# Flamingo gated block on one core: the heads' sums leave through DRAM untransposed, and their division is done for eight heads at a time

## The chip, the cores and the metric

The kernel runs on one core of one Trainium2 chip. The metric is the device time of one execution in microseconds (us). A core has a matrix engine (TensorE, "PE"; its weight loads, "PEld", overlap its matmuls), three engines for elementwise work (VectorE "DVE", ScalarE "ACT", GpSimd "POOL"), and a queue that issues transfers (SyncE, "SP"); they run at the same time and wait for each other by semaphores. The matmuls read SBUF and write PSUM, of which there are eight banks of 128 x 512 float32.

## The reference

Four sequences of 512 tokens with 256 channels go through gated attention and a gated mixture of experts. Cut to what matters here:

```python
xn = layernorm(x)
for each of 4 sequences and 16 heads (D = 16 channels each):      # 64 heads
    y  = softmax(q  k^T  * scale + causal) @ v                      # 512 keys
    y += softmax(qc kc^T * scale) @ vc                              # 1601 keys of the context
x  = x + tanh(g_xattn) * (concat(y) @ Wp + bp)
xn = layernorm(x)
out = x + tanh(g_ffn) * (shared_expert(xn) + sum of the top 2 of 7 routed experts, weighted)
expert(h) = (silu(h @ g.T) * (h @ u.T)) @ d.T                       # inner width 704
```

Each softmax has its own denominator, so a head ends with two numerators and two denominators for each of its 512 queries.

## The kernel before

**Stages.** The preparation (0 to 138 us) makes the queries and keys of all heads as stacks of three bfloat16 pieces and stores them to DRAM (`q_parts`, `k_parts`). The head loop (138 to 923) does the 64 heads one after the other. Then come the turning of y, the projection, the residual, the second layernorm, the shared expert and the routing, and the routed experts.

**A head step.** Scores are computed with keys on partitions and queries along the free axis, in eight groups (L651, L654). ACT exponentiates each group (L993). The values phases (L669) multiply the exponentials by a stack of values with a column of ones, in four groups of 32 PSUM partitions: three groups sum parts of the cross attention, the fourth the self attention. So after a head, PSUM bank 6 holds on partitions 32q to 32q+15 the numerators of part q (a channel each), and on partition 32q+16 its denominator, along 512 queries. `sums_out` (ACT, L974) copies that bank to `osb` in SBUF.

**The division, per head.** `norm` (PE, four transposes, L718) turns `osb` so that queries lie on partitions; `norm_out` (ACT, L982) copies it out; `cross_sums` (POOL, L1133 and L1135) adds the three cross parts; `reciprocals` (DVE, L1326) inverts the 128 x 8 denominators; `head_output` (POOL, L1125 and L1128) multiplies and writes the head's 16 columns of y into `shared`. After the last head, 32 transposes (L540) and eight ACT copies (L1015) bring y into the layout that the projection (L760) wants, channels on partitions: `xnT`.

**Maxima of the next heads.** A softmax needs a maximum ahead of its exponentials. PE computes bounding score pieces of the two following heads, 16 "max pieces" a head (L551 to L566), and DVE reduces each (L1242). From the first half of a head's pieces and the second, `max_parts` (DVE, L1254 to L1260) makes the row of maxima; it is transposed by PE (`rows`, L592), copied by ACT into `rowst` (L953), and put by an SP transfer (`rows_load`, L471) into the stack from which the scores of the next head are made. The pieces, `norm` and `rows` take turns in a ring of three PSUM banks (`ENTRIES`, `RING`); each waits until what used its bank three entries ago is evacuated (`bank_free`).

**Order.** Every engine has its program written out by hand. `PE_ORDER` sets PE's order in a step: with group 3 of the scores come values phase 0 and `norm`, with group 5 come `rows` and values phase 1. `run_steps` writes steps 0 and 1, a loop of 15 turns of four heads, and two more steps. SP issues, once the scores of a head are done, six transfers for the stack of the head four further on (L461), then `rows_load`.

## Time and profile before

| | us |
|---|---|
| median of 3 runs | 1413.0 (1412.93 to 1413.5) |
| the profiled execution | 1413.27 |
| its span in the trace | 1411.5 |
| PE busy in the span | 1368.6 |
| DVE, ACT, POOL busy | 880.9, 727.3, 365.4 |

The span is that of the trace from the first to the last instruction; the time that is reported contains 1.8 us more. Busy times of different engines overlap. An engine that is busy the whole span has to lose work, or to lose waits, for the time to fall; for the others it only matters when they finish what is waited for.

### The profile page before, as it was taken

The numbers are of one execution on the slowest core, as the hardware profiler recorded it, in microseconds if no ns is written. First come the engines' busy times: TensorE is split into PE (matmuls) and PEld (weight loads), VectorE is DVE, ScalarE is ACT, GpSimd is POOL, SyncE is SP. The second block draws the span as 40 slices with busy tenths as digits, with TensorE's granted clock in tenths as the row PEclk, the third lists the DMA queues.
The fourth block names the chain that finished last, engine by engine and source line by source line (L and its number), as shares of the span: only waits on it lengthen the run. The fifth ranks groups of instructions, "written<-read, shape, count | busy, mean of one in ns | idle before, by whom it ended". The sixth has DMA issues, their size and how long they took to land.

```text
span 1411.5 us, 27301 instructions
## 1 busy us (share of the span) xinstructions
PE 1368.6 (97%) x7688; PEld 694.0 (49%) x7689; DVE 880.9 (62%) x1804; ACT 727.3 (52%) x1107; POOL 365.4 (26%) x743
## 2 busy tenths in 40 slices
PE   7988999999999999999999999989999999999997
PEld 4544333333333333333333333364556777777775
DVE  6776888888888888888888888653532222222221
ACT  4644667677777676767676767732210222222221
POOL 5655222222222222222222222200001232233232
PEclk9999999999999999999999999999999999999999
DMA  8754111111111111111111111057004122112111
GB/s 246 237 186 154 43 53 51 48 50 48 47 49 50 51 50 50 49 48 48 48 51 51 50 49 50 7 218 297 0 1 134 26 33 34 30 30 37 30 30 23
DMA packets 57711, 98.43 MB, mean 70 GB/s; under 512 B 7441, under 2 KB 42001, under 8 KB 56657
## 3 DMA queue, kind: packets, MB, share of 16 engines
q1 hardware_dynamic: 50384, 88.10, 18.8%
q0 software_dynamic: 7296, 9.97, 4.5%
q8 instruction: 15, 0.25, 0.1%
q14 instruction: 16, 0.12, 0.0%
HBM read 69.20 MB, written 28.58 MB: 69 GB/s over the span
## 4 chain that ended last, share of the span: by engine, by line
PE 88%; DMA 2%; DVE 2%; ACT 1%; issue 1%; POOL 1%; SPq 0%; POOLq 0%; ACTq 0%; DVEq 0%
PE ps L669 19%; PE ps L834 13%; PE ps L651 13%; PE ps L551 13%; PE ps L847 7%; PE ps L786 5%; PE ps L797 3%; PE ps L718 3%; PE ps L654 2%; PE ps L565 2%; PE ps L858 2%; DMA k_parts<-work 2%; PE ps L555 1%; PE ps L592 1%; PE ps L625 1%
## 5 line engine op out<-in xcount | busy, mean ns | idle before, releaser
L1242 DVE TENSOR_REDUCE mx<-ps 128x1 f32<-128x512 f32 (+1 forms) x832 | 515.1, 662 | 99.6 <-PE ps L551 69.3
L993 ACT ACTIVATE arena<-ps 128x1024 f32<-128x1024 f32 (+1 forms) x512 | 484.3, 995 | 138.7 <-PE ps L651 135.2
L669 PE MATMUL ps<-arena 128*32 128x512 f32 (+5 forms) x2432 | 290.9, 525 | 0.6 <-ACT arena L993 0.4
L551 PE MATMUL ps<-arena 96*128 96x512 bf16 x768 | 263.0, 382 | 7.3 <-DMA arena<-k_parts 2.9
L651 PE MATMUL ps<-arena 98*128 98x512 bf16 x832 | 264.4, 381 | 5.0 <-DMA arena<-rowst 4.9
L1144 POOL TENSOR_SCALAR_AFFINE_SELECT arena<-arena 128x128 f32<-128x128 f32 x256 | 74.8, 292 | 439.2 <-ACT arena L993 429.3
L834 PE MATMUL ps<-arena,work 128*128 x608 | 186.4, 460 | 0.6 <-issue 0.6
L551 PEld LDWEIGHTS ps<-arena 96*128 96x128 bf16 x768 | 74.1, 96 | 178.0 <-DVE mx L1242 103.2
L1520 DVE TENSOR_TENSOR work<-work,ps 128x352 f32<-128x352 f32 x76 | 39.6, 521 | 179.1 <-ACT work L1061 179.1
L834 PEld LDWEIGHTS ps<-arena,work 128*128 128x128 f32 x608 | 112.5, 190 | 57.4 <-issue 1.1
L1242 DVE TENSOR_REDUCE mneg<-ps 128x2 f32<-128x512 f32 (+2 forms) x192 | 112.4, 640 | 23.9 <-PE ps L561 23.4
L1061 ACT ACTIVATE work<-ps 128x352 f32<-128x352 f32 x76 | 35.2, 463 | 164.6 <-PE ps L834 164.6
L1186 POOL DMA_INDIRECT out<-bv,slot_table x38 | 59.9, 1575 | 207.3 <-DVE bv L1526 197.5
L669 PEld LDWEIGHTS ps<-arena 128*32 128x32 f32 (+1 forms) x2432 | 56.6, 108 | 113.1 <-issue 110.5
L651 PEld LDWEIGHTS ps<-arena 98*128 98x128 bf16 x832 | 76.5, 98 | 66.2 <-DMA arena<-rowst 6.1
L847 PE MATMUL ps<-arena,work 128*128 (+1 forms) x456 | 105.0, 379 | 0.8 <-ACT work L1067 0.8
L847 PEld LDWEIGHTS ps<-arena,work 128*128 128x128 f32 (+1 forms) x456 | 83.6, 190 | 11.4 <-issue 1.1
L1176 POOL DMA_INDIRECT wp<-xn_rows,slot_table x38 | 37.7, 993 | 173.5 <-DVE slot_table L1509 137.7
L1066 ACT ACTIVATE work<-ps 128x256 f32<-128x256 f32 x76 | 29.0, 382 | 99.7 <-PE ps L858 99.6
L786 PE MATMUL ps<-xnT,arena 128*128 128x512 f32 x176 | 77.1, 595 | 0.4 <-DVE work L1352 0.4
L654 PE MATMUL ps<-arena 98*128 98x512 bf16 (+3 forms) x256 | 66.1, 299 | 0.0
L1526 DVE TENSOR_SCALAR bv<-ps,router 128x256 f32<-128x256 f32 x38 | 18.4, 484 | 64.1 <-PE ps L847 64.1
(161 smaller groups left out, 1406.8 us busy)
## 6 DMA issues: line engine op xcount, KB each, us to landing
arena<-in_experts SPq DMA_DIRECT2D x8, 2176.0 KB, 12.2
arena<-k_parts SPq DMA_DIRECT2D x64, 198.1 KB
arena<-k_parts SPq DMA_DIRECT2D x64, 132.1 KB
arena<-q_parts SPq DMA_DIRECT2D x64, 96.0 KB
k_parts<-work SPq DMA_DIRECT2D x16, 300.0 KB, 5.2
q_parts<-work SPq DMA_DIRECT2D x12, 384.0 KB, 5.4
arena<-k_parts SPq DMA_DIRECT2D x64, 66.0 KB
arena<-q_parts SPq DMA_DIRECT2D x64, 64.0 KB
```

Of the source, the lines that this page charges most:

```text
L551: mm = pe.matmul(out, qx[:, qt * P:(qt + 1) * P], ks[0:KROWS, T + j * CHUNK:T + (j + 1) * CHUNK], start=True, stop=True)
L651: mm = pe.matmul(bk[:, 0:w], kst[r][0:KROWS + MROWS, T + kt * P:T + (kt + 1) * P], qst[r][0:KROWS + MROWS, 1, :], start=True, stop=True)
L654: mm = pe.matmul(bk[:, o0:o0 + w], kst[r][0:KROWS + MROWS, kt * P:(kt + 1) * P], qst[r][0:KROWS + MROWS, 0, kt * P:T], start=True, stop=True)
L669: mm = pe.matmul(ps[32 * q:32 * q + VW, 6, b0:b1], vst[0:kn, r % VR, TT + kt if cross else kt, :], pr[0:kn, c0:c0 + b1 - b0], start=(phase ...
L718: mm = pe.transpose(out[:, t * P:(t + 1) * P], osb[:, t * P:(t + 1) * P], ident[:, :])
L786: mm = pe.matmul(ps[:, 2 * (k0 % 2) + j, :], wgus[:, k, w0:w0 + P], xnT[:, k, tb * T:(tb + 1) * T], start=(k == 0), stop=(k == 1))
L834: mm = pe.matmul(ps[:, 2 * c + j, 0:CH], xgT[:, b, k, :], weights[:, bass.ds(e, 1), o:o + CH], start=(k == 0), stop=(k == 1))
L847: mm = pe.matmul(ps[:, 4, 0:C], hidT[0:m, it, :], weights[0:m, bass.ds(e, 1), o:o + C], start=(it == 0), stop=(it == IT - 1))
L993: act.activation(pr[:, c0:c0 + n], ps[:, 2 * (g % 2):2 * (g % 2) + 2, :].rearrange("p b n -> p (b n)")[:, 0:n], ACT.Exp, scale=SCALE).then ...
L1144: pool.affine_select(out=exps, in_=exps, pattern=[[1, P]], compare_op=ALU.is_ge, fill=0.0, base=0, channel_multiplier=-1).then_inc(S["mask ...
L1186: pool.indirect_dma_start(out=a["out"], out_offset=bass.IndirectOffsetOnAxis(slot_table[:, i, 1:2], 0), in_=yt[:, i % 2, :], in_offset=Non ...
L1242: return dve.tensor_reduce(m, out, AX_X, ALU.max)
```

## The change

1. `norm`, `norm_out` and the per-head `cross_sums`, `reciprocals` and `head_output` are gone. The entry of `norm` in the ring of banks stays as `spare`, so that no other piece changes its bank.
2. After each head, SP stores `osb` (256 KB) to a DRAM buffer `o_parts`; the next `sums_out` waits for that store (`o_written`).
3. Once for eight heads (which are 128 channels of one sequence, thus half of the projection's input), SP loads from `o_parts`: `parts_load`, eight transfers, four for the denominators as 128 x 32 tiles ("compactly": 8 heads x 512 queries on 128 partitions) and four for the numerators, 128 channels x 512 queries, one of them straight to the place of y in `xnT`. POOL adds the cross parts (`den_sums`, `num_sums`), DVE inverts the 128 x 64 denominators (`reciprocals`), SP stores them to DRAM (`recip_store`) and loads them again repeated over the 16 channels of each head (`recip_load`), and POOL makes y with three 128 x 512 operations (`outputs`). These steps lie in different heads of the next group: the load after the group's last head's `rows_load`, then `SUMS_IN` = 5, `RECIP_IN` = 6 and `OUT_IN` = 7.
4. Steps 0 to 3 are written out, then a loop of 7 turns of eight heads, then four steps more.
5. y is made in the projection's layout, so the 32 transposes and eight copies after the last head are gone, and the projection of sequences 0 to 2 stands right behind the last values phase; its sequence 3 waits for the last group's division. The order of PE there becomes: `project(0..2)`, `turn_xn(0)`, `shared_up(0)` pieces 0 to 3, `project(3)`, pieces 4 and 5, `turn_xn(1..3)`. ACT now issues the load of the shared expert and one store of normalised rows; SP issues the last group's transfers ahead of those of the routed experts.
6. The first `rows_load` is issued within the last stores of the preparation and no longer behind them.

```diff
 def schedule():
...
         if g == 3:
-            out += [("values", 0), ("norm",)]
+            out += [("values", 0), ("spare",)]
...
+GH = P // D
+NGRP = NU // GH
+BEGUN = GH // 2
+TURNS = NGRP - 1
+SUMS_IN, RECIP_IN, OUT_IN, RECIP_AT = 5, 6, 7, 3
...
 def run_steps(eng, step):
-    step(0, 0, False, True, True)
-    step(1, 1, True, True, True)
-    heads = NR
-    turns = (NU - 2 - 2) // heads
-    with eng.Fori(0, turns) as i:
-        for h in range(heads):
-            step(i * heads + (h + 2), (h + 2) % NR, True, True, True)
+    for u in range(BEGUN):
+        step(u, u % NR, u > 0, True, True)
+    with eng.Fori(0, TURNS) as i:
+        for h in range(GH):
+            step(i * GH + (BEGUN + h), h % NR, True, True, True, i, h)
...
@@ block.sync
+                if s == ROWS_LOAD_AT:
+                    rows_load(0, 0)
...
-            rows_load(0, 0)
...
+            def sums_store(v):
+                sp.wait_ge(S["o_evac"], v + 1)
+                sp.dma_start(o_parts[bass.ds(v, 1)].rearrange("a p t -> (a p) t"), osb).then_inc(S["o_written"], 16)
+            def parts_load(j):
+                sp.wait_ge(S["parts_free"], j + 1)
+                sp.wait_ge(S["o_written"], j * (16 * GH) + 16 * GH)
+                heads = o_parts[bass.ds(j * GH, GH)]
+                for q in range(4):
+                    src = heads[:, VW * q + D:VW * q + D + 1, :].rearrange("u a (d t) -> (u a) d t", t=DW)
+                    sp.dma_start(den[:, q, :], src).then_inc(S["parts_in"], 16)
+                for q, dst in enumerate([yT[:, bass.ds(j, 1), :].rearrange("p a t -> p (a t)"), *cross_num, self_num]):
+                    sp.dma_start(dst, heads[:, VW * q:VW * q + D, :]).then_inc(S["parts_in"], 16)
...
+                    stack_loads(i * GH + (BEGUN + NR + h), h % NR)
+                    sums_store(i * GH + (BEGUN + h))
+                    if h + 1 == OUT_IN:
+                        recip_load(i)
+                    rows_load(i * GH + (BEGUN + h + 2), (h + 2) % NR)
+                    if BEGUN + h == GH - 1:
+                        parts_load(i)
+                    if h + 1 == RECIP_IN:
+                        recip_store(i)
...
@@ block.tensor
-            def norm(u):
-                pe.wait_ge(S["o_evac"], u)
-                for t in range(TT):
-                    mm = pe.transpose(out[:, t * P:(t + 1) * P], osb[:, t * P:(t + 1) * P], ident[:, :])
...
-            pe.wait_ge(S["y_done"], NU)
-            for n in range(8):
-                layer_turn(ps[:, n % 4, :], b, k).then_inc(S["y_turned"], 1)
...
@@ block.scalar
             def sums_out(u):
                 act.wait_ge(S["pv_done"], u * NPH)
+                if not (isinstance(u, int) and u == 1):
+                    act.wait_ge(S["o_written"], u * 16 - 16)
...
@@ block.gpsimd
+            def outputs(j):
+                y = group_out(j)
+                pool.wait_ge(S["recip_in"], j * 32 + 32)
+                pool.tensor_tensor(y, y, cross_recip, ALU.mult).then_inc(S["y_cross"], 1)
+                pool.tensor_tensor(self_num, self_num, self_recip, ALU.mult).then_inc(S["y_self"], 1)
+                pool.tensor_tensor(y, y, self_num, ALU.add).then_inc(S["y_done"], 1)
```

On PE, in a step of the head loop, between values phase 0 and the max piece behind it, there stands before (L669 values, L718 `norm`, L551 a max piece, L651 scores):

```order
L669 MATMUL ps<-arena 32x512 x4
L577 REGISTER_ALU
L718 MATMUL ps<-ident,work 128x128 x4
L577 REGISTER_ALU
L551 MATMUL ps<-arena 128x512
L682 REGISTER_ALU
L651 MATMUL ps<-arena 128x512 x2
```

and now (L731 values, L614 a max piece, L713 scores):

```order
L731 MATMUL ps<-arena 32x512 x4
L641 REGISTER_ALU
L614 MATMUL ps<-arena 128x512
L744 REGISTER_ALU
L713 MATMUL ps<-arena 128x512 x2
```

Only the four transposes and one register operation are gone; the order of the rest of the step is the same, down to `rows` (now L654) and beyond.

On SP, at the step of the loop in which a group of eight is complete, there stood before, behind the six stack loads (the last one is shown), the `rows_load` and then the next stack loads:

```order
L461 DMA arena<-k_parts 16x2113
L470 REGISTER_ALU
L471 DMA arena<-rowst 2x8x128
L507 REGISTER_ALU
L461 ISA
L461 DMA arena<-q_parts 48x1x1024
```

and now the beginning of what stands there (L524 the store of the sums, L487 `rows_load`, L533 the loads of the denominators in `parts_load`, of which there are four):

```order
L524 DMA o_parts<-work 128x512
L487 DMA arena<-rowst 2x8x128
L528 REGISTER_ALU
L529 ISA
L533 ISA
L533 DMA work<-o_parts 128x1x32
L533 ISA
L533 DMA work<-o_parts 128x1x32
```

The rows above are the first two of the eight loads. The end of the same place, with the last two of the four numerator loads (L535) and the first load of the next stack (L477):

```order
L535 DMA shared<-o_parts 128x1x512
L535 ISA
L535 DMA work<-o_parts 128x1x512
L559 REGISTER_ALU
L477 ISA
L477 DMA arena<-q_parts 48x1x1024
```

The eight loads of a group come between the `rows_load` of one head and the stack loads of the next, where nothing stood before.

On PE behind the last values phase there stood before (L718 the last `norm`, L540 the transposes of y and of the normalised rows, L760 the projection, L786 the shared expert):

```order
L718 MATMUL ps<-ident,work 128x128 x4
L540 MATMUL ps<-ident,shared 128x128 x32
L760 MATMUL ps<-wp,xnT 128x256 x24
L540 MATMUL ps<-ident,shared 128x128 x8
L760 MATMUL ps<-wp,xnT 128x256 x8
L786 MATMUL ps<-xnT,arena 128x512 x22
L540 MATMUL ps<-ident,shared 128x128 x24
L786 MATMUL ps<-xnT,arena 128x512 x4
```

and now (L806 the projection, L603 the transposes of the normalised rows, L830 the shared expert):

```order
L806 MATMUL ps<-wp,xnT 128x256 x24
L603 MATMUL ps<-ident,shared 128x128 x8
L830 MATMUL ps<-xnT,arena 128x512 x16
L806 MATMUL ps<-wp,xnT 128x256 x8
L830 MATMUL ps<-xnT,arena 128x512 x6
L603 MATMUL ps<-ident,shared 128x128 x24
L830 MATMUL ps<-xnT,arena 128x512 x4
```

The last `norm` and the 32 transposes of y are gone, and the last eight matmuls of the projection moved behind 16 matmuls of the shared expert.

## Rows read from the trace of the kernel before

**Rows 1.** The page: busy us by engine (share of the span) x instructions.

```profile
PE 1368.6 (97%) x7688; PEld 694.0 (49%) x7689; DVE 880.9 (62%) x1804; ACT 727.3 (52%) x1107; POOL 365.4 (26%) x743
```

**Rows 2.** Windows: stretch, length, busy (x) by engine, PEclk, DMA share, GB/s.

```profile
150.00:900.00 750.00, 748.01 (x5129) 287.39 (x5127) 630.34 (x1222) 530.99 (x672) 178.90 (x548) 1.00 0.15 49
502.27:514.58 12.31, 12.27 (x87) 4.71 (x84) 10.26 (x20) 8.69 (x11) 2.94 (x9) 1.00 0.16 50
```

**Rows 3.** All instructions of L718, duration in ns min/median/max.

```profile
L718 PE MATMUL ps<-ident,work x256: 272/273/329, 157.9 to 924.0; 128*128 128x128 f32 x128
```

**Rows 4.** Timeline of two heads: start, length, engine, line, [idle before <-releaser].

```profile
502.69 2.54 DVE L1242 TENSOR_REDUCE mx<-ps 128x1 f32<-128x512 f32 x4 [0.32 <-PE ps L551]
...
512.41 1.75 DVE L1242 TENSOR_REDUCE mneg<-ps 128x2 f32<-128x512 f32 x3 [0.43 <-PE ps L561]
514.19 0.17 DVE L1254 TENSOR_REDUCE mneg<-mx 128x4 f32<-128x16 f32 x1
...
514.09 0.66 PE L718 MATMUL ps<-ident,work 128*128 128x128 f32 x4
...
514.58 0.38 PE L551 MATMUL ps<-arena 96*128 96x512 bf16 x1
...
515.00 2.54 DVE L1242 TENSOR_REDUCE mx<-ps 128x1 f32<-128x512 f32 x4 [0.23 <-PE ps L551]
...
516.39 0.09 PEld L592 LDWEIGHTS ps<-identb,mparts 128*16 128x16 bf16 x1 [0.30 <-DVE mx L1242]
```

**Rows 5.** Timeline of SP and PE in one head, and of the 61st.

```profile
505.11 0.68 SPq L471 DMA_DIRECT2D arena<-rowst  x1
507.15 0.77 SPq L461 DMA_DIRECT2D arena<-q_parts  x1
...
508.32 0.60 PE L651 MATMUL ps<-arena 98*128 98x512 bf16 x2
...
910.26 0.62 SPq L471 DMA_DIRECT2D arena<-rowst  x1
...
912.05 0.82 PE L651 MATMUL ps<-arena 98*128 98x512 bf16 x3 [0.30 <-DMA arena<-rowst]
```

**Rows 6.** POOL: all operations of L1111, duration in ns min/median/max.

```profile
L1111 POOL TENSOR_TENSOR x<-x,bv x16: 721/724/730, 57.3 to 117.6; 128x256 f32<-128x256 f32 x16
```

**Rows 7.** Timeline at the start of the head loop, and a window behind it.

```profile
137.54 1.03 PE L651 MATMUL ps<-arena 98*128 98x512 bf16 x2 [4.56 <-DMA arena<-rowst]
...
130.80 0.53 SPq L490 DMA_DIRECT2D k_parts<-arena  x1
...
134.16 0.74 SPq L471 DMA_DIRECT2D arena<-rowst  x1
...
138.67 1.28 ACT L993 ACT_TABLE_LOAD   x1 [6.41 <-PE ps L651]
...
137.50:146.00 8.50, 8.34 (x31) 3.02 (x31) 4.67 (x10) 5.16 (x5) 0.99 (x3) 0.50 0.22 69
```

**Rows 8.** Timeline of PE from the end of the last values phase on.

```profile
923.66 0.63 PE L718 MATMUL ps<-ident,work 128*128 128x128 f32 x4 [0.80 <-ACT work L974]
926.84 5.35 PE L540 MATMUL ps<-ident,shared 128*128 128x128 f32 x32 [2.55 <-POOL shared L1128]
932.03 3.19 PE L760 MATMUL ps<-wp,xnT 128*128 128x256 f32 x14
...
970.10 3.60 PE L786 MATMUL ps<-xnT,arena 128*128 128x512 f32 x8
```

**Rows 9.** An issue of SP's after the heads, and the window behind it.

```profile
954.58 3.41 SPq L523 DMA_DIRECT2D out<-shared  x1
...
959.00:974.00 15.00, 15.00 (x56) 7.63 (x58) 2.75 (x4) 5.46 (x11) 0.00 (x0) 1.00 1.04 429
```

**Rows 10.** DMA queues (packets, MB, share of 16 engines), 210 to 900, then 900 to 915 us.

```profile
q1 hardware_dynamic: 13914, 33.42, 15.1%
...
q8 instruction: 1, 0.02, 0.5%
```

In the first of these two answers q1 is the only queue.

More of the change, by code:

```diff
@@ L117 @@
 PE_ORDER = schedule()
-ENTRIES = [item for item in PE_ORDER if item[0] in ("max", "norm", "rows")]
+ENTRIES = [item for item in PE_ORDER if item[0] in ("max", "spare", "rows")]
 RING = 3
@@ new lines, in _ @@
+            for u in range(BEGUN):
+                sp.wait_ge(S["qk_done"], NG * (u + 1))
+                stack_loads(u + NR, u % NR)
+                sums_store(u)
+                rows_load(u + 2, (u + 2) % NR)
+            with sp.Fori(0, TURNS) as i:
+                for h in range(GH):
+                    sp.wait_ge(S["qk_done"], i * (GH * NG) + NG * (BEGUN + h + 1))
+                    stack_loads(i * GH + (BEGUN + NR + h), h % NR)
[7 more added lines that the diff above has]
+                        recip_store(i)
@@ L514, in _ @@
+            for u in range(TURNS * GH + BEGUN, NU):
+                sums_store(u)
+                if u + 2 < NU:
+                    rows_load(u + 2, (u + 2) % NR)
+            parts_load(NGRP - 1)
+            recip_store(NGRP - 1)
+            recip_load(NGRP - 1)
             sp.wait_ge(S["pv_done"], NU * NPH)
@@ L577, in bank_free @@
                         pe.wait_ge(S["max_red"], min(n, NU * NMAX - MAXED) if isinstance(n, int) else n)
-                elif before[0] == "norm" and not (isinstance(u, int) and u == 0):
-                    pe.wait_ge(S["norm_evac"], step)
                 elif before[0] == "rows":
@@ L973, in sums_out, with step @@
                 act.wait_ge(S["pv_done"], u * NPH)
+                if not (isinstance(u, int) and u == 1):
+                    act.wait_ge(S["o_written"], u * 16 - 16)
                 act.activation(osb[:, :], ps[:, 6, :], ACT.Copy).then_inc(S["o_evac"], 1)
-            def norm_out(u):
-                act.wait_ge(S["norm_mm"], u)
-                if not (isinstance(u, int) and u == 1):
-                    act.wait_ge(S["y_parts"], u - 1)
-                nm = bank_of("norm").rearrange("p (t q w) -> p t q w", t=TT, q=4)
-                act.activation(sums[:, :, :, :], nm[:, :, :, 0:D + 1], ACT.Copy).then_inc(S["norm_evac"], 1)
-            def step(u, r, prev, nxt, nxt2):
+            def step(u, r, prev, nxt, nxt2, group=None, h=None):
                 for g in range(NG):
@@ L1008, in _ @@
             run_steps(act, step)
+            act.wait_ge(S["qk_done"], NU * NG)
+            act.dma_start(weights[:, SHARED, :], a["experts"][SHARED]).then_inc(S["shared_load"], 16)
             sums_out(NU)
-            norm_out(NU)
-            for n in range(8):
-                b, k = divmod(n, 2)
-                act.wait_ge(S["y_turned"], n + 1)
-                act.activation(xnT[:, k, b * T:(b + 1) * T], ps[:, n % 4, :], ACT.Copy).then_inc(S["y_freed"], 1)
             def xn_out(b):
@@ L1155, in step @@
                 mask(u, 1, 2)
-                if prev:
-                    cross_sums(u)
                 mask(u, 2, TT)
-                if prev:
-                    head_output(u)
-                    pool.wait_ge(S["y_done"], u)
+                if h == SUMS_IN:
+                    den_sums(group)
+                    num_sums(group)
+                if h == OUT_IN:
+                    outputs(group)
             pool.wait_ge(S["prep_freed"], len(pieces))
@@ L1166, in _ @@
             fill_rows(NR - 1, 3 * NR)
+            pool.nop(nofuse=True).then_inc(S["parts_free"], 1)
             run_steps(pool, step)
-            cross_sums(NU)
-            head_output(NU)
+            den_sums(NGRP - 1)
+            num_sums(NGRP - 1)
+            outputs(NGRP - 1)
             def gather(i):
@@ L1383, in _ @@
                                          op0=ALU.mult, op1=ALU.add).then_inc(S["x2_ready"], 1)
+            early = NT - TT
+            for t in range(early):
+                residual(t)
                 if t >= 1:
```

184 lines of the change are left out of this document (102 added, 82 removed).

## The prediction, made before the changed kernel ran

> **What bounds the kernel now.** First the page's busy times: PE works 1368.6 of 1411.5 us, the next engine 880.9 [rows 1]. Then the windows: from 150 to 900 us, which is the head loop, PE is busy 748.01 of 750 at the full clock, DVE 630, ACT 531, POOL 179 [rows 2]. That looks like PE alone as the bound, so that a transpose taken away would be its whole time gained. The third view, the timeline of a head, says something else. The four `norm` transposes occupy PE from 514.09 to 514.58, and behind them comes max piece 8 (L551) [rows 4]. But DVE reduced the pair of pieces before from 512.41 to 514.16, goes on with `max_parts` from 514.19, and waits only 0.23 us for max piece 8, in another head 0.32; the reduction of piece 9, the second of the four that begin at 515.00, is what PE waits 0.30 us for ahead of `rows` at 516.39 [rows 4]. PE counts as busy, since matmuls lie close around, yet its step is tied once per head to a chain on DVE that began ahead of `norm`. So the loop is PE and DVE hand in hand, and PE's saving counts only as far as DVE waits. Last the ends of the loop: 4.56 us of idle PE ahead of the first head, waiting for the transfer of rows [rows 7], and the way from the last values phase to the projection [rows 8].
>
> **Term 1, 64 times no `norm`.** It takes a slot of 514.58 − 514.09 = 0.49 us [rows 4], and there are 256 transposes, four for each head [rows 3]. Upper bound: 0.49 × 64 = 31 us. If piece 8 comes 0.49 earlier, DVE can start on it right behind `max_parts`, that is, earlier by its wait less the 0.03 that DVE leaves between two operations (514.16 to 514.19 [rows 4]): 0.20 in one head of four, 0.29 in the other three, as the two rows differ. Everything after `rows` then moves by that. Mean (0.20 + 3 × 0.29)/4 = 0.27; the 62 heads that have a piece 8: 16.5 us. Lower bound, 0.20 for all: 12. I take 16.5, because the waits ahead of `norm` (DVE's 0.43 for L561) are between PE and DVE in the other direction, and removal of PE work behind L561 does not move L561 within its head.
>
> What went on beside `norm` goes too: `norm_out`, 64 `head_output` and `cross_sums`, 64 `reciprocals`. ACT is busy 8.69 and POOL 2.94 of 12.31 us, DVE 10.26 [rows 2]. I cost their removal at nothing in the loop: PE and DVE's reductions set the pace. In the last two heads, where there are no pieces, ACT sets it, and three `norm_out` less give 1.2 us (an estimate: its 272 columns take two thirds of what `sums_out` takes, 0.6).
>
> **Term 2, the new work in the loop, per group of eight heads.** DVE: one inversion of 128 x 64 instead of eight small ones, nothing. POOL: `num_sums` two and `outputs` three operations of 128 x 512 float32. The nearest row is 128 x 256 at 0.72 us [rows 6], doubled 1.44 each: 2.9 and 4.3 us in one head. POOL's own work, 2.94, loses four operations per head, and a head has 12.3, so both fit unless they hold up the mask of the next head. Nothing taken; at worst 1 us each, 14 us in all, in the range's upper part. SP: a store of 256 KB per head, waited for by nothing until 12 us later; the loop moves 49 GB/s at a DMA share of 0.15 to 0.16 [rows 2], the store and loads add 384 KB per head, 31 GB/s. Nothing.
>
> What can cost is SP's time. `parts_load` is eight issues in a row; issues here take 0.68 and 0.77 us [rows 5], so 5.4 to 6.2 us, with two register steps each perhaps 7. Before, `rows_load` was issued at 505.11 and SP was free from 505.79 to 507.15; now the loads run from 505.8 to about 512.8. Queued behind are the six stack loads (some 4.3 us at 0.72 each, for a head three steps on, so they have time), the store of the sums and then `rows_load`: 512.8 + 4.3 + 0.7 = 517.8 against 517.4 (505.11 + 12.31). Its slack: issued at 505.11, used by PE at 508.32; where PE did wait for it, from issue to PE's start it took 1.8 us (910.26 to 912.05) [rows 5]; so 3.2 − 1.8 = 1.4 us. A lateness of 0.4 is hidden, and as issues may be longer I put up to 1 us for each of 7 groups into the sum's small terms below, with 7 as the bound. `recip_load`, two issues ahead of a `rows_load`, ends by about 514.5 on the same scale, ahead of 517.4: nothing. If it is late, POOL's `outputs` wait, and behind them the next head's masks.
>
> **Term 3, the start.** PE begins at 137.54, 4.56 us idle, when the rows issued at 134.16 are there; ACT loads its table at 138.67 after 6.41 us idle; and the clock is at 0.50 from 137.5 to 146 [rows 7], the lower of its two levels, 1.2 GHz. The rows were ready long ahead of it; now their transfer goes in front of the last stores of the preparation. Then PE can start when the maxima pieces end, and ACT's scratch buffers are bound by the store issued at 130.80 [rows 7], which lands near 134.4 (an estimate: 3.6 us from its issue, as PE's wait shows 3.4 for the rows), plus 1.28 us of table: exponentials from about 135.7 instead of 139.97 (138.67 + 1.28): 4.2 us. PE's idle stretch shrinks from 4.56 to some 2.3, and before the stretch the clock was at full; if it stays there, the first 8.5 us run at it: PE was busy 8.34 of them at half, but DVE 4.67 and ACT 5.16, which the clock leaves alone, so I take 1.8 of at most 4.2. Together 6.0; bounds 4.2 and 8.
>
> **Term 4, from the last values phase to the shared expert.** Before: the values end at about 922.8; then `norm` at 923.66, 0.80 us after PE's last matmul, POOL's chain (PE idle 2.55 to 926.84), 32 transposes for 5.35, projection at 932.03 [rows 8]. Now the projection of sequences 0 to 2 starts where the values end: 9.3 earlier. Its tiles are paced by DVE as before. To the first matmul of the shared expert's second sequence, 970.10 [rows 8], nothing else is removed, and the moved `project(3)` gives PE work in between, where DVE's residuals and normalisations set the pace either way. Gain 9.3. The end of the last group's division is the cover to look at: the store of the last sums is issued when `sums_out` ends, 923.6, and all that follows is estimated at 3 us from issue to landing and 0.5 us an issue: landed 926.6, eight loads to 933, POOL and DVE to 936, store and load of the reciprocals to 942, POOL's three operations (4.3) to 946.3; `project(3)` is due 27 us after 922.8, near 950. Slack 3.5 us. Hence nothing, and if it were 3 us longer, still nothing.
>
> Behind it SP starts the experts' loads (before right behind the last values phase) only at about 941, and they, with the stores of normalised rows, saturate the engines (share 1.04, 429 GB/s [rows 9]). DVE reuses the memory of the normalised rows in the shared expert and so waits for the stores to land. The stores' arrival there (estimate 968, as before) is just where it was needed, so I take no loss. Bounds: 0 and the whole 9.3.
>
> **Sum.** −6.0 − 16.5 − 1.2 − 9.3 = −33.0. For small lateness of rows and POOL, +2. The profiled execution took 1413.27 (span 1411.5 and 1.8 outside of it), the median 1413.0, so the forecast is 1413.0 − 31.0 = 1382.
>
> **The rivals.**
> *DVE is not in the way* (0.07). The pieces ahead of `norm` shift too, and PE gives all 0.49 per head: 31 in place of 16.5, thus 1413 − 48 + 2 ≈ 1367. For it: PE busy 99.7%. Against it: DVE's chain from 512.41 is gapless up to piece 8 but for 0.23.
>
> *A stall at the loop's turn* (0.13). The loop body becomes eight heads long. From 210 to 900 us only data queues moved anything, and from 900 to 915, where the loop ends, one fetch of instructions of 0.02 MB shows, 0.5% of 16 engines for 15 us, that is 1.2 us [rows 10]: the body of four heads was held. A body of eight may not be, and each of the 6 turns back would wait for one or more fetches; at 1.5 to 3 us a turn that is 9 to 18 us, thus 1391 to 1400. The Trainium skill, "Runtime: NRT & Kernel Launch" (Instruction fetch mechanics), gives PE 128 KiB and the others 32 KiB, and says that a taken branch outside that window stalls until the target is fetched. By it an estimate of 100 KB for PE's body still fits, and DVE's 21 KB fits if it lies well.
>
> *The transition's gain is eaten* (0.10). The experts' loads start 18 us later and reach the stage where DVE or PE waits for the stores. Price up to 9.3: 1391.
>
> *Slower than before* (0.07). The loads of `parts_load` fetch small pieces and their issues are not 0.7 but as long as the one of 3.41 us that SP needed with full queues [rows 9]: 8 × 3.41 = 27.3 us of SP, against 6.6 free between two `rows_load` (11.6 less the stack loads and the store) and 1.4 of slack. Then `rows_load` comes 19.3 us late 7 times, 135 us, and the time is 1413 − 31 + 135 = 1517. It decides from 31/7 = 4.5 us a group on, thus from (8.0 + 4.5)/8 = 1.6 us for each issue, where the time is 1413. For it: that row. Against: in the loop, with queues at a share of 0.16 [rows 2], the issues are at 0.68 and 0.77 [rows 5].
>
> **How the numbers follow.** 0.63 for the forecast, 1375 to 1388 for it alone (start ±2, heads ±4, rows and POOL up to 5 more). Above it the range goes to the loop's stall and the eaten transition, 1398, and below to the gain of all bounds but the first rival's, 1373. A difference of 0.2%, 2.8 us, is about what a measurement can tell. Faster 0.90: all cases but the last, 0.93, less 0.02 for a stall of 5 us a turn and 0.01 for issues close to the 1.6, which both end within 0.2%, so same is 0.03; slower 0.07.
>
> **What the changed profile would show.** Pitch of heads 12.04 instead of 12.31; DVE without the wait on the max piece behind the values phase, PE still waiting some 0.1 to 0.3 for L1242 ahead of `rows`; first scores at about 134 to 135 and PEclk above 0.5 there; projection starting at once behind the values; no PE wait for the rows' transfer in any eighth head. I am wrong if the loop shortens by under 10 or over 25 us, if a PE gap of over 1 us appears once per eight heads, or if the shared expert waits for DMA.

## The result, and the profile after

The changed kernel takes 1501.0 us (1498.2 to 1502.3) beside 1413.25 of the kernel before on the same chip: ratio 1.0615, 95% interval 1.0597 to 1.0634. It is 88 us slower, and the forecast was 1382. The page of the changed kernel, where it answers to [rows 1] and, for the fetches of instructions of the whole execution, [rows 10]; then the chain that ended last, and the stores of the sums (KB, us to landing):

```profile
PE 1375.0 (92%) x7400; PEld 670.4 (45%) x7401; DVE 881.8 (59%) x1748; ACT 699.5 (47%) x1037; POOL 332.3 (22%) x543
...
PEclk9999999899899899899899899999999999999999
...
q8 instruction: 20, 0.33, 0.1%
...
PE 66%; DMA 14%; SPq 5%; issue 4%; DVE 4%; ACT 3%; POOL 0%; POOLq 0%; DVEq 0%; ACTq 0%
...
o_parts<-work SPq DMA_DIRECT2D x64, 256.0 KB, 7.1
```

PE is no longer busy all the time, transfers have 14% of the chain that ended last, and PEclk dips in a regular beat. So the first thing to look at is what repeats once per group of eight heads. PE's row for the transposed maxima (L654) comes once per head; from the timeline of the changed kernel, the starts of four of them:

```profile
251.96 0.22 PE L654 MATMUL ps<-identb,mparts 128*16 128x128 bf16 x1 [0.16 <-DVE mx L1297]
...
274.07 0.22 PE L654 MATMUL ps<-identb,mparts 128*16 128x128 bf16 x1
...
285.98 0.22 PE L654 MATMUL ps<-identb,mparts 128*16 128x128 bf16 x1 [0.16 <-DVE mx L1297]
...
303.66 0.22 PE L654 MATMUL ps<-identb,mparts 128*16 128x128 bf16 x1 [0.24 <-DVE mx L1297]
```

These are four heads in a row, with distances of 22.1, 11.9 and 17.7 us. An undisturbed head takes 11.91 on average, where it took 12.28 before. Every group has one head of 22.1 to 23.1 us and, two heads on, one of 15.4 to 18.1. Over 11.91 the first kind adds 74 us in seven groups and the second 38: 112 us. What PE waits for in them, from the timeline of the changed kernel, [idle before <-releaser] last (the first row shows a max piece, from before the wait):

```profile
255.89 0.39 PE L614 MATMUL ps<-arena 96*128 96x512 bf16 x1
264.28 1.03 PE L713 MATMUL ps<-arena 98*128 98x512 bf16 x2 [8.00 <-DMA arena<-rowst]
...
292.59 1.01 PE L713 MATMUL ps<-arena 98*128 98x512 bf16 x2 [2.29 <-DMA arena<-rowst]
```

Both are waits for the transfer of the rows. SP's issues in the same stretch:

```profile
240.86 0.69 SPq L487 DMA_DIRECT2D arena<-rowst  x1
243.59 3.14 SPq L533 DMA_DIRECT2D work<-o_parts  x4
246.95 0.65 SPq L535 DMA_DIRECT2D xnT<-o_parts  x1
247.80 1.45 SPq L535 DMA_DIRECT2D shared<-o_parts  x2
249.44 0.62 SPq L535 DMA_DIRECT2D work<-o_parts  x1
250.33 0.79 SPq L477 DMA_DIRECT2D arena<-q_parts  x1
...
254.35 0.32 SPq L477 DMA_DIRECT2D arena<-k_parts  x1
254.85 0.39 SPq L524 DMA_DIRECT2D o_parts<-work  x1
255.28 0.68 SPq L487 DMA_DIRECT2D arena<-rowst  x1
...
282.99 1.42 SPq L549 DMA_DIRECT2D work<-recip_rows  x2
286.82 0.70 SPq L487 DMA_DIRECT2D arena<-rowst  x1
```

The eight loads of a group take 0.60 to 0.79 us each to issue, as forecast. SP begins them only at 243.59, 2.0 us after it was free, because the last store of sums takes 7.1 us to land. So the rows' transfer is issued at 255.28 and not at 252.8 (240.86 + 11.94), 2.5 us late. That alone, against 1.4 of slack, would cost 1.1. But from its issue to PE's start it takes 9.0 us, where it took 1.8 before [rows 5]. The windows of that time, clock share, DMA share and GB/s last:

```profile
252.00:256.00 4.00, 4.00 (x26) 1.15 (x26) 3.53 (x6) 2.71 (x4) 0.58 (x2) 1.00 0.55 187
256.00:260.00 4.00, 0.28 (x1) 0.00 (x0) 0.72 (x2) 0.00 (x0) 2.98 (x4) 0.80 0.29 107
260.00:264.00 4.00, 0.00 (x0) 0.00 (x0) 0.00 (x0) 0.00 (x0) 0.00 (x0) 0.50 0.28 93
```

While PE waits, the 16 DMA engines are together at a share of 0.28: most are idle, and the transfer of 4 KB waits all the same. That is the finding which the experiments are about.

The waits are not the whole of the 112 us. PE is idle for the rows 8.2 us on average in the first kind of head and 2.5 in the second, 75 us in all 14. The other 37 us are about what the clock takes: at its upper level in the head before, it is at 0.50 (1.2 GHz) when PE starts again, and PE works at it for some 4 us after the first wait and 7 us after the second. The windows around the second wait, in the same form:

```profile
288.00:292.00 4.00, 2.30 (x14) 0.51 (x12) 2.74 (x5) 1.94 (x2) 0.00 (x0) 1.00 0.16 54
292.00:296.00 4.00, 3.41 (x12) 1.14 (x15) 1.51 (x3) 1.68 (x2) 3.54 (x3) 0.57 0.28 90
296.00:300.00 4.00, 4.00 (x27) 1.51 (x20) 1.02 (x3) 1.58 (x3) 0.93 (x3) 0.58 0.14 55
```

Two matmuls of L713, which take 0.60 us at the upper level (as L651 in [rows 5]), take 1.03 and 1.01 in the two rows above. So the head of 17.7 us is 5.8 too long with a wait of only 2.3.

The end of the heads, where [rows 8] has the kernel before, PE and then DVE:

```profile
1009.42 10.96 PE L806 MATMUL ps<-wp,xnT 128*128 128x256 f32 x48
...
1036.73 8.77 PE L830 MATMUL ps<-xnT,arena 128*128 128x512 f32 x16 [7.18 <-DVE work L1408]
...
1056.74 3.60 PE L830 MATMUL ps<-xnT,arena 128*128 128x512 f32 x8
...
1030.02 0.55 DVE L1379 RECIPROCAL work<-work 128x64 f32<-128x64 f32 x1 [8.21 <-POOL work L1161]
```

The projection does start at once behind the values, but from there to the shared expert's second sequence it is 1056.74 − 1009.42 = 47.3 us, the same as before from the end of the values (922.8 to 970.10 [rows 8]). DVE stands 8.2 us at the last group's inversion, with all later tiles behind it.

### The profile page after: what moved, and what is told of

The parts are those of the page before. It is cut to its first block, busy times and chain, and to the rows that moved or that the text cites. A ratio compares the mean times of both kernels' runs of the same rounds, so it can differ in the third digit from the quotient of the medians.

```text
span 1499.8 us, 26182 instructions
## 1 busy us (share of the span) xinstructions
PE 1375.0 (92%) x7400; PEld 670.4 (45%) x7401; DVE 881.8 (59%) x1748; ACT 699.5 (47%) x1037; POOL 332.3 (22%) x543
## 4 chain that ended last, share of the span: by engine, by line
PE 66%; DMA 14%; SPq 5%; issue 4%; DVE 4%; ACT 3%; POOL 0%; POOLq 0%; DVEq 0%; ACTq 0%
PE ps L731 13%; PE ps L878 12%; PE ps L713 9%; PE ps L614 8%; DMA arena<-rowst 7%; PE ps L891 7%; PE ps L830 5%; DMA o_parts<-work 4%; PE ps L841 3%; SPq L477 2%; PE ps L902 2%; ACT arena L1032 2%; SPq L533 2%; SPq L535 1%; PE ps L716 1%
## 5 line engine op out<-in xcount | busy, mean ns | idle before, releaser
L713 PE MATMUL ps<-arena 98*128 98x512 bf16 x832 | 274.1, 393 | 78.3 <-DMA arena<-rowst 76.3
L731 PE MATMUL ps<-arena 128*32 128x512 f32 (+5 forms) x2432 | 303.1, 543 | 0.6 <-ACT arena L1032 0.6
L614 PE MATMUL ps<-arena 96*128 96x512 bf16 x768 | 272.9, 395 | 6.7 <-DMA arena<-k_parts 2.4
L614 PEld LDWEIGHTS ps<-arena 96*128 96x128 bf16 x768 | 76.1, 99 | 232.8 <-DVE mx L1297 102.7
L713 PEld LDWEIGHTS ps<-arena 98*128 98x128 bf16 x832 | 76.5, 99 | 145.9 <-issue 80.2
L731 PEld LDWEIGHTS ps<-arena 128*32 128x32 f32 (+1 forms) x2432 | 58.6, 111 | 127.6 <-issue 124.0
L830 PE MATMUL ps<-xnT,arena 128*128 128x512 f32 x176 | 79.0, 605 | 8.0 <-DVE work L1408 7.2
L716 PE MATMUL ps<-arena 98*128 98x512 bf16 (+3 forms) x256 | 69.4, 312 | 0.0
L1021 ACT ACTIVATE work<-ps 128x512 f32<-128x512 f32 x64 | 38.2, 597 | 50.2 <-PE ps L731 50.2
```

What stands on the lines that cost most here:

```text
L614: mm = pe.matmul(out, qx[:, qt * P:(qt + 1) * P], ks[0:KROWS, T + j * CHUNK:T + (j + 1) * CHUNK], start=True, stop=True)
L713: mm = pe.matmul(bk[:, 0:w], kst[r][0:KROWS + MROWS, T + kt * P:T + (kt + 1) * P], qst[r][0:KROWS + MROWS, 1, :], start=True, stop=True)
L716: mm = pe.matmul(bk[:, o0:o0 + w], kst[r][0:KROWS + MROWS, kt * P:(kt + 1) * P], qst[r][0:KROWS + MROWS, 0, kt * P:T], start=True, stop=True)
L731: mm = pe.matmul(ps[32 * q:32 * q + VW, 6, b0:b1], vst[0:kn, r % VR, TT + kt if cross else kt, :], pr[0:kn, c0:c0 + b1 - b0], start=(phase ...
L830: mm = pe.matmul(ps[:, 2 * (k0 % 2) + j, :], wgus[:, k, w0:w0 + P], xnT[:, tb, k, :], start=(k == 0), stop=(k == 1))
```

## The experiments

Where no range is given, an experiment is one run; four runs of one of these kernels lay between 1375.2 and 1380.7 us, so differences of a few us are read from the traces and not from the times.

Theory Q: transfers that SP issues are worked off in order on the DMA engines that they share. The stack loads of a head keep two or three engines busy (by the DMA share) for some 9 us. In the kernel before they were issued early and the rows 6 us behind the last one; now the loads of a group push them right ahead of the rows' transfer, which waits for them. Rival B: the group's own megabyte holds the engines. Rival I: the rows' transfer is only issued too late.

**Without the groups' work.** For seven of eight groups the loads, sums, inversions, reciprocals' transfers and outputs are left out.

```diff
-                    if h + 1 == OUT_IN:
-                        recip_load(i)
...
-                    if BEGUN + h == GH - 1:
-                        parts_load(i)
-                    if h + 1 == RECIP_IN:
-                        recip_store(i)
...
-                if h == SUMS_IN:
-                    den_sums(group)
-                    num_sums(group)
-                if h == OUT_IN:
-                    outputs(group)
```

> Leaves out, for seven of the eight groups, the loads of the parts, the sums, the reciprocals with their store and load, and the outputs (the heads' division); the store of each head's sums and the last group stay. Every theory of the stalls says that the two long heads of each group go: in the changed kernel they add 74 us (heads of 22 to 23 us) and 38 us (heads of 15 to 18 us) over a pitch of 11.9, so 1501 - 112 = 1389 us, with a pitch of 11.9 throughout. If heads above 13 us remain, the store alone is part of the cause.

Measured: 1390.4 us beside the 1389 expected, the heads of the loop at 11.86 to 12.03 but for one of 12.7. The stores of all heads' sums stay in, and cost the loop nothing. The 112 us are the groups' work.

**Loads and sums only.**

```diff
-                    if h + 1 == OUT_IN:
-                        recip_load(i)
...
-                    if h + 1 == RECIP_IN:
-                        recip_store(i)
...
-                    outputs(group)
+                    pool.nop(nofuse=True).then_inc(S["parts_free"], 1)
```

> Leaves out, for seven groups, the store and load of the reciprocals and the outputs; the eight part loads, the sums and the inversion stay. If the two stalls of a group are independent, the first (74 us over seven groups) stays and the second (38 us) goes: 1463 us. If the second is an echo of the first, it stays: 1501 us.

Measured: 1470.5 us. Each group has one long head, of 22.0 to 24.9 us, and no second. The two stalls are independent. The second belongs to what this run leaves out; that it is `recip_load`, which stands ahead of a rows' transfer in the same way, and not the stores or outputs left out with it, is argued from the order of SP's issues. The time is 7.5 us above the expected 1463, 5 of them because the first stalls are longer here (79 us in all).

**Same issues, few bytes.**

```diff
-                    sp.dma_start(dst, heads[:, VW * q:VW * q + D, :]).then_inc(S["parts_in"], 16)
+                    sp.dma_start(dst[:, 0:D], heads[:, VW * q:VW * q + D, 0:D]).then_inc(S["parts_in"], 16)
```

> The four numerator loads of a group keep their place and number, but bring 16 columns instead of 512 (the sums are then taken over stale columns): 1 MB less per group, the same issues. Theory Q (the rows' transfer waits in SP's queue behind the six stack loads that now stand right ahead of it; these need about 9 us on the few DMA engines they use): the stall of 8.0 us stays nearly whole, at least 6 us, total 1485 to 1501. Rival B (the group's own bytes hold the engines): the first stall falls to 1 or 2 us, total about 1435. Rival I (only the late issue of the rows' transfer counts, 2.5 us late against 1.4 of slack) gives about 1 us of stall in this and in the changed kernel, which its trace already speaks against.

Measured: 1475.0 us, below the 1485 of the expectation. PE's wait is 4.8 to 7.1 us, 6.2 on average, where it was 8.2; in three of the seven groups it is under the 6 that were expected at least. The long heads are at 19.5 to 21.8 us, 8.6 above 11.91 on average; with all bytes it was 10.6. Three quarters of the wait and four fifths of the stall have nothing to do with the group's megabyte: B falls, and Q keeps the larger part. Numerators ahead in the queue cost the other 2 us.

**Rows issued by ACT.** 

```diff
                         rows(u + 1, bank_of("rows"))
+                        act.wait_ge(S["rows_evac"], u + 2)
+                        act.dma_start(qst[(r + 1) % NR][KROWS:KROWS + MROWS, :, :].rearrange("p i t -> p (i t)"), rowst[:, :]
+                                      ).then_inc(S["rows_ready"], 16)
```

> Nothing left out. The transfer of the rows is issued by ACT right behind the copy that makes them, on ACT's own queue, and no longer by SP. Theory Q: a queue of its own does not wait behind SP's stack loads, both stalls go, 1501 - 105 = 1396 us, less what ACT's issue of 0.4 to 0.7 us per head costs (ACT idles 1.2 us there). If the transfer must wait for the busy DMA engines whichever queue it is in, the stalls stay at 4 us or more and the time above 1440 us.

Measured: 1452.1 us. It is the second case of the expectation by the time (above 1440) and by the first stall: the long heads fall to 16.3 to 18.8 us, 4.4 to 6.9 above 11.91, and the others to 12.6 to 15.9. The rows' transfer of such a head and PE's start on it, from this run's timeline:

```profile
251.29 0.63 ACTq L1045 DMA_DIRECT2D arena<-rowst  x1
...
257.48 0.60 PE L715 MATMUL ps<-arena 98*128 98x512 bf16 x2 [2.72 <-DMA arena<-rowst]
```

The issue at 251.29 is in time, and yet PE starts 6.2 us later, not 1.8. I (late issue) explains none of this. The 6.2 can't be set against the 9.0 as what a second queue is worth: this issue comes 4 us earlier than SP's did, when SP has not issued the last two stack loads and the store. What it shows is that a queue of its own does not take the transfer past all that is in front; that an engine which it needs is itself taken is the reading, and the next runs test it.

**Stack loads on 16 engines.** Then the engines. The loads name their rows with an outer count of 3, 2 or 1 (pieces); with the 16 channels outside it is 16, with the same bytes in the same rows. The rows of queries and of keys change place in the same way, so that their products are summed in another order and nothing else.

```diff
-                sp.dma_start(dst, src.rearrange("a d i t -> (a i) d t")).then_inc(stack[r], 16)
+                sp.dma_start(dst, src.rearrange("a d i t -> (a d) i t")).then_inc(stack[r], 16)
```

> Nothing left out. In the changed kernel, the six stack loads of a head name their rows as 16 channels of up to 3 pieces each instead of up to 3 pieces of 16 channels: same bytes, packets and issues, but an outer count of 16. Theory Q (with an outer count of 3, 2 or 1 these loads lie on few DMA engines, two or three at a time by the share of 0.13 to 0.19, and whatever SP issues next waits behind them for some 9 us): the stack loads are through in 2 to 3 us, the rows' transfer comes 2 to 3 us after its issue, and of both stalls only the late issue is left, 1 to 2 us each: 1501 - 112 + 14 to 28 = 1403 to 1417 us. Rival: how the rows of a load are named does not matter, or the group's own 1 MB on eight engines holds the rows up: stalls as before, 1480 to 1501 us.

Measured: 1406.4 us, 95 us less than the changed kernel by one line. The second stall is gone (11.91 there), the first is at 1.2 to 6.1 us a group, 28 in all; another 9.6 come before the second head's `rows`. The store of the sums, which was behind the stack loads too, lands after 2.1 us and not 7.1; the page's issues in this run (KB, us to landing):

```profile
o_parts<-work SPq DMA_DIRECT2D x64, 256.0 KB, 2.1
```

The page also counts the packets, here for the changed kernel and then for this run:

```profile
DMA packets 80119, 128.70 MB, mean 86 GB/s; under 512 B 15504, under 2 KB 50064, under 8 KB 79056
DMA packets 83575, 128.71 MB, mean 92 GB/s; under 512 B 18960, under 2 KB 53520, under 8 KB 82512
```

The 3456 more are all under 512 B, 54 for each of 64 heads.
**The same line in the kernel before.**

> The kernel before with the same one edit, stack loads with an outer count of 16. Theory Q: there the stack loads end before the rows' transfer is issued, so it gains nothing in the loop: 1411 to 1413 us. If the loop of the kernel before had hidden waits for the rows, it falls.

Measured: 1405.9 us beside 1413.6, not the 1411 to 1413 expected. The heads are at 12.23 to 12.31 as ever: in the loop of the kernel before nothing waited for this. The 7.4 us come from the preparation, where the first stack loads stand among the stores of pieces. Windows from 66 to 104 us, in the kernel before (busy times by engine, clock share, DMA share, GB/s):

```profile
66.00:104.00 38.00, 30.26 (x101) 16.15 (x101) 27.02 (x60) 16.30 (x31) 20.82 (x23) 1.00 0.63 205
```

The same window in this run:

```profile
66.00:104.00 38.00, 35.96 (x130) 20.55 (x129) 32.45 (x71) 18.17 (x35) 24.73 (x27) 1.00 0.73 226
```

PE does 130 matmuls there instead of 101. So some 7 of the 95 us that the line takes off the changed kernel have nothing to do with the change.

**An inversion per head added.** To find why a head gained 0.37 us and not 0.27.

```diff
                         for i in range(3):
                             max_parts(u + 1, i)
+                    if prev and c == HALF + 4:
+                        dve.wait_ge(S["dve_extra"], u)
+                        dve.reciprocal(rsum8[:, 0:8], rsum8[:, 8:16]).then_inc(S["dve_extra"], 1)
```

> The run without the groups' work (1390.4 us, pitch 11.91), with one inversion of 128 x 8 on DVE added back in each head, at the place where the kernel before had it. The heads gained 0.37 us each, not the 0.27 of the prediction. Theory: the rest, 0.10, came from this inversion of 0.19 us, because DVE is in the chain that sets the pitch: pitch 12.0, total about 1396 us. Rival: it came from ACT's or POOL's lost work: pitch 11.91, 1390 us.

Measured: 1400.0 us. The pitch (the time from head to head) stays at 11.86 to 11.94 in most heads, so my theory falls. The 10 us are somewhere else: one head of each turn of the loop takes 13.6 to 13.8 us instead of 12.03. DVE's waits in this run from 150 to 880 us (in total, times, longest):

```profile
DVE mx L1288 <- issue: 13.6, 6, 2.4
```

Fetches of instructions on one queue from 150 to 900 us (packets, MB, share), this run:

```profile
q14 instruction: 39, 0.32, 0.1%
```

and the same of the run without the inversions:

```profile
q14 instruction: 9, 0.07, 0.0%
```

DVE stands 6 times, 2.3 us each, waiting for nothing in the program, and there are 30 more fetches of 8 KB. The trace has five of these fetches in each turn, at the same place of it: in one turn two begin at 279.8 and 280.6, and DVE stands from 280.5 to 282.8. This is the rival of the loop's turn, made to happen: a body of eight heads with eight more inversions and their waits has to be fetched again in part at each turn. In the changed kernel itself there is no fetch of instructions at all from 290 to 960 us.

**No last group either.** The last group's transfers, sums, inversion and outputs are left out as well, and DVE waits for the last store of sums instead.

```diff
-            parts_load(NGRP - 1)
-            recip_store(NGRP - 1)
-            recip_load(NGRP - 1)
...
-                if t == 9:
-                    reciprocals(NGRP - 1)
```

> As the run without the groups' work, and the last group's loads, sums, inversion, store, load and outputs are left out too. Theory: the transition gained nothing because the last group's chain ends 6.7 us too late for project(3) and holds up DVE (8.2 us) ahead of it; without it PE gets from the last values phase to the shared expert's second sequence in 38 us instead of 47.3: 1390.4 - 9.3 = 1381 us. Rival: the arrival of the shared expert's weights or DVE's tiles set this stage: less than 3 us gained.

Measured: 1381.6 us, 8.8 under the 1390.4, but 2.4 of this are at the start (the third `rows` at 155.2 and not 157.7), and one long head of the other run is missing. From the projection's start to the shared expert's second sequence it is 936.73 − 894.63 = 42.1 us, in its timeline:

```profile
894.63 10.96 PE L796 MATMUL ps<-wp,xnT 128*128 128x256 f32 x48
...
918.35 7.13 PE L820 MATMUL ps<-xnT,arena 128*128 128x512 f32 x16 [3.60 <-DVE work L1386]
...
936.73 3.60 PE L820 MATMUL ps<-xnT,arena 128*128 128x512 f32 x8
```

So with no last group the stage gains 5.2 us on 47.3, between theory (9.3) and rival (under 3); PE still waits 3.6 for DVE's tiles.

**Both edits, the loads spread, and the best.** Three kernels with stack loads on 16 engines. The first has the rows issued by ACT as well; the second spreads a group's numerator loads, two each over the next two heads, and gives the denominators a semaphore of their own; the third run is the second with the rows issued by ACT:

```diff
                     if BEGUN + h == GH - 1:
                         parts_load(i)
+                    if BEGUN + h == GH:
+                        nums_load(i, 0, 2)
+                    if BEGUN + h == GH + 1:
+                        nums_load(i, 2, 4)
```

> Both edits together: stack loads over 16 engines, and the rows' transfer issued by ACT on its own queue. With the first edit alone 1406.4 us are left, with one stall per group of 1 to 6 us, 28 us over seven groups, where the rows' transfer, issued on time, takes 5 us to arrive behind the numerator loads. If the order within SP's queue is what holds it, a queue of its own ends it: 1378 us. If the eight DMA engines are taken by the numerator loads for every queue alike, 10 us or more of the 28 remain: 1388 us or more.

> Nothing left out. Stack loads over 16 engines; a group's four denominator loads where they were, but its numerator loads two each in the next two heads, behind the rows' transfer; the denominators have a semaphore of their own, so that their sum does not wait for the numerators (also in the last group). Theory Q: with 2.7 us of numerator packets on an engine instead of 5.4, ahead of stack loads that need 2 us, the rows' transfer is no longer late: the 28 us of stalls go. In the last group the inversion comes some 8 us sooner, so that the transition gains 5 to 9 us: 1406.4 - 28 - 7 = 1371 us, between 1367 and 1382.

> The run before with the rows' transfer issued by ACT on its own queue as well. If the spread loads have ended the stalls, it changes nothing or costs a little of ACT's time: 1371 to 1375 us. If stalls of 1 us or more were left, it takes them away.

Measured: 1375.0; 1378.2 (1375.2 to 1380.7), ratio to before 0.9755 (0.9736 to 0.9774); 1378.3 (1377.4 to 1383.3), ratio 0.9766 (0.9746 to 0.9787), above the 1371 to 1375 expected of it. In the first every head is at 11.8 to 12.0: once the engines are free, a queue of its own takes away the rest of the stall, so what was left was order within SP's queue behind the numerators. Spreading the loads does it too. But the spread loop has a head of 12.5 us at each turn instead of 12.03. It is not a fetch again: there is none from 290 to 840 us. PE's waits in the second run from 139 to 860 us (in total, times, longest):

```profile
PE ps L741 <- POOL arena L1208: 3.9, 7, 0.6
```

L741 is the values, L1208 POOL's mask. This run moved POOL's two sums of the numerators into the head that also has `outputs`; five operations of 1.27 us stand there ahead of the mask, and PE waits 0.6 us for it in each of seven groups.

The last kernel has stack loads on 16 engines and the rows issued by ACT, and keeps all eight loads together, with the own semaphore:

```diff
-            pool.wait_ge(S["parts_in"], j * 128 + 128)
+            pool.wait_ge(S["parts_in"], j * 64 + 64)
...
                 y = group_out(j)
+                pool.wait_ge(S["nums_in"], j * 64 + 64)
```

> Nothing left out. Stack loads over 16 engines, rows' transfer by ACT, all eight loads of a group at one place, and a semaphore of its own for the denominators. The run without that last edit took 1375.0 us with a loop free of stalls; the run with spread loads showed 3.4 us less between the last values phase and the end of the shared expert, where the inversion no longer waits for the numerators, but 0.5 us more at each turn of its longer loop. So 1375.0 - 3.4 = 1371.6 us, between 1369 and 1375.

Measured: 1372.8 us (1372.3 to 1373.8), ratio to before 0.9717 (0.9704 to 0.9731). From the values to the second sequence it takes 928.62 − 884.86 = 43.8 us:

```profile
884.86 10.97 PE L808 MATMUL ps<-wp,xnT 128*128 128x256 f32 x48
...
906.07 7.13 PE L832 MATMUL ps<-xnT,arena 128*128 128x512 f32 x16 [1.08 <-DVE work L1414]
915.43 5.41 PE L808 MATMUL ps<-wp,xnT 128*128 128x256 f32 x16 [2.22 <-POOL xnT L1192]
...
928.62 3.60 PE L832 MATMUL ps<-xnT,arena 128*128 128x512 f32 x8
```

Beside the kernel before with the same line for its stack loads (1405.9, one run) this is 33 us: 7 at the start of the heads, 23 in the heads, 3 behind them. That this is near the 31 of the forecast is partly luck, since its terms were 6.0, 17.7 and 9.3.

## Why the prediction was wrong

The account of the changed kernel against the one before, from both traces: −3.4 at the start (the first `rows` of the loop at 144.6 instead of 148.0), −23 for 62 heads at 0.37, +112 for the stalls (75 of waits, 37 at the lower clock), +1 at the loop's turns and in the last heads, 0 in the transition, +1.7 behind it (1056.74 to the routed experts' first matmul 119.0 us, before 117.3): +88; measured 88. Of the prediction's own signs of being wrong, a gap of over 1 us on PE once per eight heads came, twice over.

- **Term 2, the step that failed.** "From issue to PE's start it took 1.8 us; so 3.2 − 1.8 = 1.4 us." That was taken where the stack loads had long been issued, and was used as a constant, while the same paragraph pushed the stack loads right ahead of the transfer. SP's time was right (0.60 to 0.79 an issue, 2.5 us late with the wait for the store); what a queue still has to carry when SP is free again was left out. The rows in front of me gave no more than a hint: a DMA share of 0.15 for 49 GB/s [rows 2] is a mean of 2.4 engines busy, and says nothing of how it is spread over 16. In the changed kernel the same transfer takes 9.0 us from issue to PE's start in one head and 5.8 (286.82 to 292.59) in another. And the price of a wait was put at its own length: with the clock it is 10.2 us for a wait of 8.0 and 5.8 for one of 2.3. The changed kernel's first stall of 10.6 us on average is 8.6 without the bytes of the numerators, and about 4 once the stack loads are spread.
- **`recip_load`, "nothing".** It stands just ahead of a rows' transfer, and the stall there costs 38 us in seven groups, by the same mechanism as far as is shown; with the stack loads on 16 engines it costs nothing, so the price was right for its own issues and wrong for what stands ahead of them.
- **The store of the sums, "waited for by nothing until 12 us later".** It lands 7.1 us after its issue, behind the stack loads, and `parts_load` begins 2.0 us after SP is free for that reason; with the store landed after 2.1 us it was 0.4, and the rows were issued in time (230.89 and then 242.83).
- **The rival "slower than before"** (0.07) had the sign and the place, but another mechanism: issues of above 1.6 us. None of a group's eight was above 0.79. Its point of decision, 4.5 us beyond the slack per group, holds: there were 16.
- **Term 1** was 0.37 instead of 0.27 a head. DVE's wait for piece 8 went, as said (0.23 and 0.32 to 0.00, the 0.03 between operations too, which is 0.30). The other 0.07 stay open; it was not the inversion on DVE.
- **Term 3**: 3.4 instead of 6.0. PE's first score moved from 137.54 to 134.20 and the exponentials from 139.97 to 136.90, 3.1 of the 4.2; the clock was at 0.71 from 137.5 to 146. But the first `rows` of all came 1.4 us later here than before (117.1 and 115.75); the other runs with this preparation have 116.2 to 117.7, and why is not shown.
- **Term 4**: 0 instead of 9.3. The chain was put at 23.5 us from the end of the values, and took 33.6: the last store has landed 7.2 us in, not 3.8, and all eight loads at 20, not 10.2. ACT issues the shared expert's 2.2 MB ahead of that store, which may be why; it was not tried by itself. And its end was compared only with `project(3)`, not with the inversion on DVE, which sits in the middle of the tiles. Even with no last group it would have given 5.2.
- **The loop's turn** (0.13) did not stall in the changed kernel: no fetch from 290 to 960 us, and in the last kernel, where nothing covers it, the head at the turn has 12.02 us instead of 11.94. The rule of the Trainium skill, "Runtime: NRT & Kernel Launch" (Instruction fetch mechanics), that a taken branch whose target is not in the window of two pages waits for a fetch, agrees in kind with the run with the added inversions, at 1.6 us of pitch a turn. For PE the prediction took the window to be its 128 KiB, where the rule speaks of two pages of 16 KiB; the trace fits the prediction, since PE's body of eight heads, which it put at 100 KB (an estimate), comes round without a fetch.

## What to carry to other kernels

When a change puts transfers into a queue, ask what the queue still has to carry ahead of each latency-critical small one, and on how many engines, not only when the issuer is free: here the six loads ahead took 9 us while the DMA engines stood at a share of 0.28. What helped here was an outer count of 16 for the big transfers (95 us) and then a queue of its own for the small one that gates a step (31 us). A latency read from a trace holds for the neighbours it had there; if the change moves them, it is no longer a bound.

## What the runs showed of the hardware that was not expected

- The outer count of a transfer decides how long it holds up what stands behind it: with 3, 2 and 1 the store behind the six loads landed after 7.1 us, with 16 after 2.1, at the same bytes. In the kernel before the same line gave 7.4 us. The Trainium skill, "DMA: Bandwidth & Descriptors" (Why a DMA increments its semaphore by 16 and not by 1), states that the slowest dimension that is not 1 sets the number k of engines, and that the lowest-numbered k are taken. The first agrees with the 54 small packets more a head, a count of 1 being passed over for the 16 behind it. The second would put the four loads with counts of 3 and 2 and the rows' transfer on the same two or three engines, which no view here shows, as none names an engine.
- A second queue passes what is in front only in part: with the rows on ACT's queue, issued in time, PE still started 6.2 us after the issue while the stack loads lay on few engines. With these on 16 engines the same step ended the rest: the waits of 1.1 to 3.4 us behind the numerators on SP's queue (1406.4 us) went to none on ACT's (1375.0).
- A short wait of PE can cost more by the clock than by itself: 2.3 us idle, then 6.8 us at 0.50, and a head 5.8 us longer.
- Eight small operations more in a loop body on DVE cost 1.6 us at each turn, with 30 fetches of 8 KB more over the loop.
